# A transformer block with linear attention and routed experts: the tailor's factor formed from norms, with gamma applied at its end, and an expert's bounds in three small operations

## The reference

```python
Q = x @ Wq.T + bq ; K = x @ Wk.T + bk ; V = x @ Wv.T + bv
Q = transpose(Q / norm(Q over tokens)) ; K = K / norm(K over tokens)
tailor_sum = 1.0 / (L + einsum('bnc,bc->bn', Q, sum(K, axis=-1) + EPS))      # L = 256
matrix = einsum('bmn,bcn->bmc', K, V)
matrix_sum = sum(V, axis=-1) + einsum('bnm,bmc->bcn', Q, matrix)
return x + gamma * matrix_sum * tailor_sum
```

## Time and profile before

| | us |
|---|---|
| median of 3 runs | 732.36 |
| lowest and highest | 729.3 and 732.49 |
| profiled execution | 731.41 |
| its span, first to last instruction | 729.6 |
| VectorE busy | 458.6 (63%) |
| ScalarE busy | 458.1 (63%) |
| TensorE busy | 634.2 (87%) |
| eight rounds | about 24 to 240 of the span |

### The profile page before, as it was taken

One profiled execution on the slowest core, in us unless ns is written; L12 is line 12 of the kernel. 1 busy time (PEld: TensorE's weight loads), 2 busy tenths in 40 slices (PEclk: granted clock), 3 DMA queues, 4 the chain that ended last, 5 costly groups with the idle time before them and its releaser, 6 DMA issues.

```text
span 729.6 us, 17404 instructions
## 1 busy us (share of the span) xinstructions
PE 634.2 (87%) x5255; PEld 544.8 (75%) x5255; DVE 458.6 (63%) x1242; ACT 458.1 (63%) x879; POOL 306.4 (42%) x389
## 2 busy tenths in 40 slices
PE   4778889889888799999889999999999979999900
PEld 3666677667665588998778998998998868899800
DVE  5479988989885663535654444444444446778766
ACT  2657756757744584756647675675675547978872
POOL 4000432633527522557773353453453824534150
PEclk9989989999997999999989999999999989999965
DMA  8165364364255432112132222212111891624177
GB/s 257 64 232 189 117 186 130 137 198 149 86 174 175 118 95 67 55 35 75 33 93 75 82 81 73 80 54 73 53 53 46 164 206 46 98 65 78 41 181 165
DMA packets 46600, 79.88 MB, mean 109 GB/s; under 512 B 17905, under 2 KB 31538, under 8 KB 46130
## 3 DMA queue, kind: packets, MB, share of 16 engines
q1 hardware_dynamic: 33954, 47.17, 20.4%
q0 software_dynamic: 12560, 31.60, 17.9%
HBM read 48.96 MB, written 29.78 MB: 108 GB/s over the span
## 4 chain that ended last, share of the span: by engine, by line
PE 57%; DVE 14%; issue 9%; ACT 7%; DMA 7%; POOL 5%; ACTq 1%; DVEq 0%; SPq 0%; POOLq 0%
PE banks L467 14%; PE banks L469 14%; PE banks L468 14%; PE banks L879 3%; DMA stage<-in_L_ffn_W 2%; ACT X L1351 2%; PE banks L953 2%; PE banks L813 2%; DMA X<-y_rows 2%; PE banks L832 2%; DMA stage<-y_rows 2%; PE banks L836 1%; POOL table L707 1%; DVE zone L1547 1%; POOL X L721 1%
## 5 line engine op out<-in xcount | busy, mean ns | idle before, releaser
L1351 ACT ACTIVATE X<-banks,b1T,tab 128x256 f32<-128x256 f32 x312 | 157.0, 552 | 127.0 <-PE banks L469 93.8
L1796 DVE SCALAR_TENSOR_TENSOR stage<-X,tab,stage 128x512 f16<-128x512 f32 x156 | 116.5, 752 | 129.4 <-ACT stage L1356 121.5
L467 PE MATMUL banks<-X,W 128*128 128x256 f16 x624 | 172.2, 276 | 8.9 <-DVE X L1803 7.9
L728 POOL DMA_INDIRECT y_rows<-X,tb x78 | 88.6, 1136 | 205.2 <-DVE X L1819 185.6
L468 PE MATMUL banks<-X,W 128*128 128x256 f16 x624 | 172.1, 276 | 0.0
L469 PE MATMUL banks<-X,W 128*128 128x256 f16 x624 | 172.0, 276 | 0.0
L467 PE MATMUL banks<-W,stage 128*128 x624 | 170.8, 274 | 1.1 <-DVE stage L1796 0.8
L468 PE MATMUL banks<-W,stage 128*128 x624 | 170.7, 274 | 0.0
L469 PE MATMUL banks<-W,stage 128*128 x624 | 170.7, 274 | 0.0
L1356 ACT ACTIVATE stage<-X,tab 128x512 f16<-128x512 f32 x156 | 112.6, 722 | 11.5 <-ACT X L1351 7.5
L721 POOL DMA_INDIRECT X<-xf_rows,tb x78 | 93.3, 1196 | 32.4 <-issue 23.5
(11 more groups left out here) (273 smaller groups left out, 1020.1 us busy)
## 6 DMA issues: line engine op xcount, KB each, us to landing
stage<-in_L_ffn_W SPq DMA_DIRECT2D x16, 1024.0 KB, 7.9
X<-in_L_attn_x SPq DMA_DIRECT2D x8, 512.0 KB, 4.8
out<-X SPq DMA_DIRECT2D x8, 512.0 KB, 2.7
xf_rows<-zone SPq DMA_DIRECT2D x8, 512.0 KB, 2.9
u_rows<-b2b SPq DMA_DIRECT2D x8, 512.0 KB, 7.5
X<-y_rows POOLq DMA_DIRECT2D x8, 512.0 KB, 11.0
away<-W SPq DMA_DIRECT2D x1, 2048.0 KB, 12.0
W<-away SPq DMA_DIRECT2D x1, 2048.0 KB, 8.4
```

Source lines behind the costliest of these rows:

```text
L467: pe.matmul(o, lh, rh, start=first, stop=False)
L728: g.indirect_dma_start(out=y_rows, out_offset=bass.IndirectOffsetOnAxis(ap=tb[:, j % ROWS, h, 1:2], axis=0), in_=y32[:, j % 2 * HALVES + h ...
L1351: a.activation(h32[:, m % 2, r * BT:(r + 1) * BT], PS[m][:, r * BT:(r + 1) * BT], ACT.Gelu, bias=b1T[:, bass.ds(e * NH + 2 * m + r, 1)], s ...
L1796: v.scalar_tensor_tensor(o[1], src, tab[:, 1, bass.ds(e, 1)], o[0], ALU.mult, ALU.subtract).then_inc(h_low, 1)
```

## The change

The query norm now enters directly. Before, the factor was 1 / (m/|q| + eps qsum/|q| + 256), the mix was m gamma/|q| + gamma vsum, and both inverse norms were formed. Now the mix is m + vsum |q|, and the factor is gamma / (m + eps qsum + 256 |q|), which is the same value. So `tailor_factors` goes with its three operations, only the key norms are inverted (two columns), `tailor` has four operations instead of three, the mix reads the norm and not gamma times its inverse, and `vsum` is kept without gamma. Since the norms are read later, the query sums and the query roots of the next image wait for the tailor of this one. In the bounds the factor 2 is put into an immediate and into the square of b1 (scaled by 2), which leaves three operations.

```diff
-NORMS, TAILOR = 3, 3
+NORMS, TAILOR = 1, 4
-EV_BOUNDS, EV = 4, 9
+EV_BOUNDS, EV = 3, 8
@@ ScalarE
 def uq_out(b):
-                a.wait_ge(norm_steps, NORMS * b)
+                a.wait_ge(tailor_steps, TAILOR * b)
 def q_roots(b):
+                a.wait_ge(tailor_steps, TAILOR * b)
 def w1_square(i):
-                a.activation(bsq[:, :], b1T[:, TURN[i] * NH:(TURN[i] + 1) * NH], ACT.Square, accum_out=essq[:, 2:3]).then_inc(w1_squares, 1)
+                a.activation(bsq[:, :], b1T[:, TURN[i] * NH:(TURN[i] + 1) * NH], ACT.Square, scale=2.0, accum_out=essq[:, 2:3]).then_inc(w1_squares, 1)
@@ VectorE
             def inverses(b):
-                v.wait_ge(norms_ready, 2 * (b + 1))
+                v.wait_ge(norms_ready, 2 * b + 1)
                 v.wait_ge(cosines_ready, NF * b)
-                link(v.reciprocal(rk[:, :], kn[:, :]))
-
-            def tailor_factors(b):
-                link = chain(v, norm_steps, NORMS * b + 1)
-                v.tensor_scalar(gq[:, :], rk[:, 0:NF], gam_b[:, 0:1], None, ALU.mult).then_inc(gq_ready, 1)
-                link(v.scalar_tensor_tensor(pre[:, :], qsum[:, :], EPS_TAILOR * KAPPA, rk[:, 0:NF], ALU.mult, ALU.mult))
-                link(v.tensor_scalar(pre[:, :], pre[:, :], float(D), None, ALU.add))
+                link(v.reciprocal(rk[:, :], kn[:, NF:2 * NF]))
             def tailor(b):
-                link(v.tensor_tensor(dn[:, :], MIX_PS[:, :, D], rk[:, 0:NF], ALU.mult))
-                link(v.tensor_tensor(dn[:, :], dn[:, :], pre[:, :], ALU.add))
+                link(v.scalar_tensor_tensor(dn[:, :], qsum[:, :], EPS_TAILOR * KAPPA, MIX_PS[:, :, D], ALU.mult, ALU.add))
+                link(v.scalar_tensor_tensor(dn[:, :], kn[:, 0:NF], float(D), dn[:, :], ALU.mult, ALU.add))
                 link(v.reciprocal(dn[:, :], dn[:, :]))
+                link(v.tensor_scalar(dn[:, :], dn[:, :], gam_b[:, 0:1], None, ALU.mult))
             def mix_out(b):
-                v.wait_ge(gq_ready, b + 1)
+                v.wait_ge(norms_ready, 2 * (b + 1))
-                    v.scalar_tensor_tensor(ymix[:, n, :], MIX_PS[:, n, 0:D], gq[:, n:n + 1], vsum, ALU.mult, ALU.add).then_inc(mixed, 1)
+                    v.scalar_tensor_tensor(ymix[:, n, :], vsum, kn[:, n:n + 1], MIX_PS[:, n, 0:D], ALU.mult, ALU.add).then_inc(mixed, 1)
             def expert_bounds(i):
-                link(v.scalar_tensor_tensor(ebnd[:, 2:3], etot[:, 0:1], float(D), etot[:, 2:3], ALU.mult, ALU.add))
-                link(v.tensor_scalar(ebnd[:, 0:2], etot[:, 0:2], 1e-24, None, ALU.max))
-                link(v.tensor_scalar(ebnd[:, 2:3], ebnd[:, 2:3], 2.0, 1e-24, ALU.mult, ALU.max))
+                link(v.scalar_tensor_tensor(etot[:, 2:3], etot[:, 0:1], 2.0 * D, etot[:, 2:3], ALU.mult, ALU.add))
+                link(v.tensor_scalar(ebnd[:, 0:3], etot[:, 0:3], 1e-24, None, ALU.max))
                 link(v.reciprocal(ebnd[:, 0:3], ebnd[:, 0:3]))
@@ setup
-            v.tensor_scalar(vsum, COS_PS[:, 0:D], gam_b[:, 0:1], None, ALU.mult).then_inc(vsum_ready, 1)
+            v.tensor_copy(vsum, COS_PS[:, 0:D]).then_inc(vsum_ready, 1)
```

More of the change, by code:

```diff
@@ L105, in sandwich @@
         kn = sb("kn", [P, 2 * NF], F32)
-        rk = sb("rk", [P, 2 * NF], F32)
-        gq = sb("gq", [P, NF], F32)
+        rk = sb("rk", [P, NF], F32)
         qsum = sb("qsum", [P, NF], F32)
         qnorm = sb("qnorm", [P, NF], F32)
-        pre = sb("pre", [P, NF], F32)
         dn = sb("dn", [P, NF], F32)
@@ L368, in sandwich @@
         enter_factor = sem("enter_factor")
-        gq_ready = sem("gq_ready")
         z_dev = sem("z_dev")
@@ L1159, in cosines_out @@
                 for l in range(NF):
-                    a.activation(gk[:, l, :], COS_PS[:, l * D:(l + 1) * D], ACT.Copy, scale=rk[:, NF + l:NF + l + 1]).then_inc(cosines_ready, 1)
+                    a.activation(gk[:, l, :], COS_PS[:, l * D:(l + 1) * D], ACT.Copy, scale=rk[:, l:l + 1]).then_inc(cosines_ready, 1)
             def mix_scale(b):
@@ L1706, in step @@
                     expert_tables(i)
-                if mixing is not None:
-                    tailor_factors(mixing)
                 if leaving is not None:
@@ L1736, in last_step @@
                 inverses(b)
-                tailor_factors(b)
                 leave(b - 1)
```

## The result

The changed kernel took 735.17 us in the median of 20 runs (730.05 to 740.74), the kernel before 731.91 (729.05 to 735.12; 20 runs). The ratio is 1.0049 with a 95% interval of 1.0029 to 1.0068: slower by 3.6 us (the medians lie 3.3 apart, the means 3.5), where 1.05 was forecast. Its profiled execution took 735.18 us with a span of 733.3, before 731.41 and 729.6. Ratios and mean clocks leave out runs that lie more than 1.5% above the fastest of their kernel.

A forecast was written before the change was run, and what follows sets the result against it. VectorE's small operations between expert totals and turned tokens were taken to bound the rounds, with TensorE's mix as floor. Shifts over rounds 0 to 7 summed to +1.05 us on 731.41, giving 732.5 us, range 729.5 to 735.3.

The forecast's parts named there:

- the opening paragraph: Edits touch only the eight rounds, about 24 to 240 us; their gain or loss moves the end by as much.
- Floors and hand-overs: In the rounds, the mix starts no earlier than 0.10 us after TensorE's L862 ends, which hides the removed VectorE operations.
- The fourth operation: Tailor's added multiplication by gamma, behind the mix on VectorE, costs a slot of 0.26 us a round, bounds 0.19 to 0.50.
- The swapped mix: L1515 with SBUF first and PSUM second takes 478 ns, bounds 423 and 533, 0.9 us in all either way.
- The credits of 0.33 and 0.32 in rounds 4 and 6: In these rounds the mix L1515 can start 0.33 and 0.32 us earlier, down to the floor set by L862.
- Rival (a): In the rounds VectorE's operation count decides: each gains 0.73 and loses 0.26, 3.8 us in all, 727.6; chance 0.08.
- Rival (b): Shifted weight loads ahead of rounds 1 to 6 turn slow: 4.9 us more, 737.4 us; chance 0.08.
- Rival (c): Everything is hidden, the added operation too, as ScalarE's half of the copy holds L1557's consumer: 731.4 us; chance 0.12.

The follow-up runs named there:

- `after_again`: The changed kernel once more, beside the kernel before at 731.11 us: ratio 1.0031; its profiled execution took 729.69 us.
- `before_fourth`: The kernel before with one more waited two-column operation (dn times one) at the end of tailor: ratio 1.0041.
- `before_fill`: The kernel before with matmuls of ones, whose result nobody reads, in TensorE's idle places of the rounds: ratio 0.9969.
- second comparison: The changed kernel, unaltered, measured again beside the kernel before at 731.11 us: ratio 1.0031.
- the third: The changed kernel, unaltered, measured a third time beside the kernel before at 757.26 us: ratio 0.9997.
- first comparison: The first measurement of the changed kernel against the kernel before, medians 735.17 and 731.91 us: ratio 1.0049.
- `tailor_only`: The changed kernel with the four bounds operations and the square of b1 of the kernel before, so the tailor part alone: ratio 1.0029.
- `five_again`: The kernel before with five more waited two-column operations at the end of tailor, measured a second time: ratio 1.0392.

## Why the prediction was wrong

The direction was right, the size was not. Two steps failed. The first is in the opening paragraph: that whatever the rounds gain or lose on the path moves the end by as much and no more. The sum priced instructions and hand-overs and put TensorE's clock at nothing, without a reason; yet the prediction's own row of round 7 has the eight matmuls of the mix at 2.54 us, where rounds 1, 3 and 4 have 1.90. In the profiled pair the rounds grew by 5.6 us, with 45.7 us at half clock instead of 30.9. The first expert block began 5.8 us later (L467 at 240.66, L464 at 246.45), where about 1 was forecast, and the end came 3.7 later. The second is the size of two terms of the path, below. How much of the 3.6 us is the clock's stays open.

- Floors and hand-overs: right. The mix starts 0.10 after its matmuls, and VectorE idles where it was given time.
- The fourth operation: 0.26 was taken, and it added 0.32 a round in rounds 1 to 6, up to 0.47 in round 4, in the traces of the changed kernel and of `after_again` alike. That is 0.4 us more in all. The swapped mix: right, 477 ns.
- The credits of 0.33 and 0.32 in rounds 4 and 6: mis-sized. They rest on one execution of before, in which the mix started 0.43 and 0.42 after its matmuls, and L1498 took 0.46 in round 4. `before_fourth` and `before_fill` have the same instructions up to there, and in their traces it is 0.11 and 0.26. By these the credits are 0.01 and 0.16, 0.5 us less. With both corrections the path is about +1.9 instead of +1.05.
- Rival (a), the count of operations decides: fell. 24 fewer operations, and slower; VectorE's idling ahead of the mix took them. With it falls, for this kernel, the advice of the Trainium skill (VectorE: DVE Perf Modes, "Rules for kernel authors") to minimize the count: it holds for operations that something waits for.
- Rival (b), slower by weight loads: not what happened. The waits for W2 that were quick before (0.98, 1.05, 1.67) stayed so (0.97, 1.35, 1.68), and the slow ones became shorter. The prediction's one mechanism for more than the path was looked for in the DMA queues.
- Rival (c): fell. The row of L464 names L1550 as what it waited for.

The clock's part in the change itself is shown less well than in a longer tailor. Taken to equal clock as above, the changed kernel lies 1.6 us (within 1.1) above before in the second comparison and 0.2 (within 1.0) in the third; in the first, the clocks of before's runs are not on record. The corrected path of 1.9 fits the second and not the third. The mean clock of its runs was 0.9414 in the first comparison, where before's profiled execution had 0.944; in the second it was 0.9436 beside 0.9438, and in the third 0.9301 beside 0.9284, which is higher. `before_fourth` was 3 us slower at an unchanged mean clock, and `tailor_only` too. So of the 3.6 us, about 2 are the path as measured; what is left, some 1.7, may be the clock of those runs or the scatter between comparisons (1.0049, 1.0031, 0.9997), and no run here decides between them. That the range still held the measured time is owed to its width, not to the mechanism.

## What to carry to other kernels

A saving on an engine that then waits is worth nothing, and an operation added behind that wait costs its whole slot: sort small operations by whether they stand before or behind the join, and move those that nobody needs yet behind the hand-over. Where TensorE idles in every round and its clock falls in some of them, a delay is not priced by its length alone; read the granted clock of each stretch before making the sum, and test the price with the delay made five times as long. Matmuls of no use in the idle place show that the clock has a part, but they also take away half clock that was there before; for the size of the part compare runs at equal clock. And take no credit from a row that one execution alone has: a second trace of the same instructions shows whether it was chance.

## What the runs showed of the hardware

The clock's fall is not tied to one place behind an idling. In round 3 of `five_again` it was 1.00 through 2.8 us without a matmul, and 0.51 from 1.7 us into the next batch on, while TensorE was fully busy. In round 0 of the changed kernel it fell within the idling ahead of L867, 1.1 us before it ended:

```profile
35.50:37.90 2.40, 0.00 (x0) 0.00 (x0) 2.08 (x7) 2.40 (x2) 0.00 (x0) 1.00 0.00 0
38.00:39.10 1.10, 0.00 (x0) 0.00 (x0) 1.10 (x1) 1.05 (x3) 0.00 (x0) 0.50 0.00 0
```

Nor is it tied to every idling: see round 6 of the changed kernel and its other rounds above. Five small operations more a round cost 30 us of 760, about 17 of them by the clock (an estimate, from runs at 0.90 in the mean beside 0.925 and 0.928). The Trainium skill (Perfetto Trace Analysis, "Matmul Optimizations") says that TensorE scales its power with utilization and that matmuls should run back to back in batches; the runs agree in so far as matmuls of ones in the idle places raised the mean clock from 0.902 to 0.950. Small operations that waited for each other took slots of 0.19 to 0.20 us in round 1 of the changed kernel, the one that reads PSUM (L1498) no more than the others; the multiplication by a scalar out of a column took 254 ns in the mean at two columns, where the addition of a constant, L1500 of the kernel before, took 170.
